# First scores on other banks, fewer stack transfers, two sets of q and k parts, first row sums on PE, calls reordered

## The chip, the cores and the metric

The kernel runs on one core of one Trainium2 chip. The metric is the device time of one execution in microseconds; lower is better. Engines are called PE (TensorE), ACT (ScalarE), DVE (VectorE), POOL (GpSimd) and SP (SyncE, which here only issues DMAs). All engines run side by side and wait for each other on semaphores.

## The reference, cut to what matters

A transformer block with modulated norms, in float32, for x of 8 batches x 512 rows x 256 columns: windowed causal attention with 16 heads of 16 (a row sees itself and the 128 rows before it), a GELU block of width 1024, and a mixing block.

```python
mod = (silu(c) @ wmod).reshape(B, 6, 1, -1)          # sa, ca, ga, sb, cb, gb
h = layernorm(x) * (1 + ca) + sa
# attention block on h
a = layer_norm(h, ln1_w, ln1_b)
q, k, v = (a @ W + b).reshape(B, L, 16, 16)
scores = einsum("blhd,bmhd->bhlm", q, k) / 4 + band   # -inf outside 0 <= i - j <= 128
ctx = einsum("bhlm,bmhd->blhd", softmax(scores), v)
h = h + ctx @ Wo + bo
h = h + gelu(layer_norm(h, ln2_w, ln2_b) @ W1 + b1) @ W2 + b2
x = x + ga * h                                        # |ga| is held at 0.25 or more
# mixing block
h = layernorm(x) * (1 + cb) + sb
prev = h shifted by one row
r = sigmoid((mu_r * h + (1 - mu_r) * prev) @ W_r.T)
k = square(relu((mu_k * h + (1 - mu_k) * prev) @ W_k.T))
out = x + gb * (r * (k @ W_v.T))
```

## The kernel before

There are 8 batches (`n` or `b`) and 16 half batches. In the attention part a half batch `u` is half of the heads (8 of 16, all 512 rows); in the later parts a half batch `i` is half of the rows (256). Each engine has its own block of code with functions such as `scores(gp, first, last_)`, and then a long list of calls: the order of work on each engine is written out by hand, call by call, with a loop over batches 3 to 6 (DVE and POOL have their own bounds) in the middle. Engines only meet on semaphores. A call of a half batch that doesn't exist does nothing.

The attention of a half batch goes like this. `norm_a` (ACT) and `transposes_a` (PE) bring the normed rows into `at_hi` and `at_lo`, two float16 parts of one float32 value. `project(u)` (PE) makes q and k. `high_qk(u)` (ACT) and `low_qk(u)` (DVE) split them into `qt_hi`, `qt_lo`, `kt_hi`, `kt_lo`; k has a pair of columns for each row, one for the even and one for the odd head, so that a pair of heads shares 32 partitions. `maxima(u, 0..3)` takes all four banks of `quad`: PE multiplies the high parts alone, DVE reduces them to a bound of the row's maximum (`nmax`). `max_rows`, `max_copy`, `low_m` and `max_send` (PE, ACT, DVE, ACT's DMA) bring that into four rows of the stack `q_st`. `stacks(u, first, last_)` are DMAs from SBUF to SBUF: for each of four pairs `j` they put the parts of q and of k on top of each other, so that one product over 96 + 4 rows gives high x high + low x high + high x low less the maximum. Before, each pair takes six DMAs (three of q, three of k), and ACT issues the pairs 2 and 3 of the first two half batches, SP all others. The stacks have two buffers (`half`), the parts have one.

`scores(gp, first, last_)` (PE), with gp = 4u + j, writes four pieces, each to a bank of the ring `ring_s`, which are the four banks of `quad`; `exps` (ACT) takes the exponential of two of them at a time into one of eight `p32`; `select(gp)` (POOL) sets what lies outside the band to zero; `sums(gp)` (POOL) adds the overlapping parts of a row into `ps` (two additions). `context(u)` (PE) multiplies by the values (`v_blk`) into bank 4 and then sums the rows with `sel` into the bank `den`. `copy_den` (ACT), `fold_den`, `save_den`, `spread_den` (SP's DMAs) and `divide`, `scale_c` (DVE) apply 1/sum. Two half batches of `scale_c` complete a batch of `ct`; then `out_project`, `residual_a`, `stats_b`, `rstd_b`, `norm_b`, `transposes_b`, `up`, `gelu`, `high_f`, `low_f`, `down` and the mixing block (`transposes_d`, `receptance`, `keys`, `values_b` on PE) follow, on the rings `ring_b` (banks 6 and 7) and `ring_f` (bank 5).

A ring hands out its banks in turn, and a new user waits for the semaphore of the bank's last user. `load_v(n, half)` fills half of `v_blk` with four DMAs. `warm(n, times)` are products of the identity with itself into bank 5, whose results nobody reads. The weights are prepared at the start by the functions `setup_...`. `hold` is a wait that is left out where an earlier wait of that engine covers it.

## Time and profile before

| | us |
|---|---|
| median of 3 runs (643.40 to 646.79) | 643.89 |
| the profiled execution | 644.62 |
| its span, first to last instruction | 642.9 |
| PE busy | 579.4 (90%), 6494 products |
| DVE busy | 418.7 (65%) |
| ACT busy | 449.8 (70%) |
| POOL busy | 384.1 (60%) |
| mean granted clock of PE | 0.975 of 2.4 GHz |

How to read it: products on PE overlap, so PE busy is not PE at its peak. The filler products of `warm` count as busy (L229, 322 products, 49.7 us, two for each `times`). The share of busy time is an average over a start in which the weights are prepared and the first batches come in, a repeating middle and an end. DMAs are not in the busy times; a "q" behind an engine's name (SPq, ACTq) is its issuing side.

### The profile page before, as it was taken

Reading aid. Unit: us, or ns where it says so; the run is one execution under the profiler, and the core shown is the slowest. Engines: PE = TensorE matmul, PEld = TensorE weight load, DVE = VectorE, ACT = ScalarE, POOL = GpSimd, SP = SyncE. Lnnn points to the kernel's source line nnn. Section 1 sums busy time; section 2 is a strip of 40 time slices with the busy share of each in tenths; the row PEclk is TensorE's granted clock in tenths of the full one; section 3 lists DMA queues with packets and bytes.
Section 4 is the critical chain, followed back from the end, with each engine's and each line's share of the span. In section 5 each row is a group of like instructions: output and inputs, shape, how many; then the busy total and the mean of one; then the engine's idle time right before and its main releaser. Section 6 shows DMA issues by size and latency. Waiting matters only on the chain.

```text
span 642.9 us, 16628 instructions
## 1 busy us (share of the span) xinstructions
PE 579.4 (90%) x6494; PEld 454.9 (71%) x6494; DVE 418.7 (65%) x847; ACT 449.8 (70%) x758; POOL 384.1 (60%) x610
## 2 busy tenths in 40 slices
PE   5888888799889999989998999999899989999986
...
GB/s 239 194 92 128 84 58 52 86 68 102 112 115 53 79 57 69 124 91 104 57 136 83 112 44 112 108 114 47 94 97 95 51 97 44 93 36 34 34 42 33
DMA packets 63516, 55.74 MB, mean 87 GB/s; under 512 B 14459, under 2 KB 52669, under 8 KB 63438
## 3 DMA queue, kind: packets, MB, share of 16 engines
...
q14 instruction: 27, 0.22, 0.1%
...
## 4 chain that ended last, share of the span: by engine, by line
PE 52%; DVE 16%; ACT 14%; SPq 5%; POOL 5%; issue 4%; DMA 3%; ACTq 0%; DVEq 0%; POOLq 0%
PE bank L351 4%; DVE nmax L1519 4%; PE bank L468 4%; PE quad L330 3%; PE bank L456 3%; PE bank L480 3%; PE bank L429 3%; PE bank L430 3%; PE bank L431 3%; PE quad L380 3%; PE bank L229 3%; ACT bank L1021 3%; SPq L2536 2%; SPq L2538 2%; PE quad L257 2%
## 5 line engine op out<-in xcount | busy, mean ns | idle before, releaser
L970 ACT ACTIVATE p<-quad,scale_s 128x768 f32<-128x768 f32 (+1 forms) x90 | 73.3, 825 | 17.4 <-PE quad L330 16.0
L2151 POOL TENSOR_SCALAR_AFFINE_SELECT p<-p 128x448 f32<-128x448 f32 x64 | 40.3, 630 | 73.9 <-ACT p L975 45.6
L1519 DVE TENSOR_REDUCE nmax<-quad 128x8 f32<-128x1032 f32 x64 | 78.9, 1233 | 2.2
L1021 ACT ACTIVATE bank<-bank,bias,scale_g 128x256 f32<-128x256 f32 x128 | 63.1, 532 | 17.3 <-PE bank L414 17.1
L412 PE MATMUL bank<-bt_hi,w_hi 128*128 128x256 f16 x256 | 70.3, 275 | 4.1 <-DVE hid_lo L1579 4.0
L429 PE MATMUL bank<-w_hi,hid_hi 128*128 128x256 f16 x256 | 69.9, 273 | 1.4 <-DVE hid_lo L1579 0.9
L413 PE MATMUL bank<-bt_lo,w_hi 128*128 128x256 f16 x256 | 69.9, 273 | 0.0
L414 PE MATMUL bank<-bt_hi,w_lo 128*128 128x256 f16 x256 | 69.8, 273 | 0.0
L431 PE MATMUL bank<-w_hi,hid_lo 128*128 128x256 f16 x256 | 69.8, 273 | 0.0
L430 PE MATMUL bank<-w_lo,hid_hi 128*128 128x256 f16 x256 | 69.8, 273 | 0.0
L2166 POOL TENSOR_TENSOR ps<-p 128x384 f32<-128x384 f32 x64 | 65.2, 1019 | 3.1 <-PE quad L363 1.3
L330 PE MATMUL quad<-q_st,k_st 100*128 100x192 f16 (+3 forms) x576 | 57.7, 231 | 9.9 <-ACT p L970 4.4
L1579 DVE SCALAR_TENSOR_TENSOR hid_lo<-bank,inv_f,hid_hi 128x512 f16<-128x512 f32 x64 | 47.2, 745 | 21.8 <-ACT hid_hi L1031 21.4
L2168 POOL TENSOR_TENSOR ps<-ps,p 128x320 f32<-128x320 f32 x64 | 56.9, 889 | 5.0
L330 PEld LDWEIGHTS quad<-q_st,k_st 100*128 100x128 f16 x576 | 41.2, 98 | 23.3 <-issue 5.1
L975 ACT ACTIVATE p<-quad,scale_s 128x288 f32<-128x288 f32 (+1 forms) x76 | 36.8, 541 | 19.8 <-PE quad L330 19.7
L1516 DVE COPY_PREDICATED quad<-later,quad 128x248 f32<-128x248 int16 x64 | 26.7, 416 | 36.7 <-PE quad L296 36.6
L229 PE MATMUL bank<-ident 128*128 128x128 f32 x322 | 49.7, 309 | 0.3 <-DVE peak L1732 0.3
L229 PEld LDWEIGHTS bank<-ident 128*128 128x128 f32 x322 | 44.2, 216 | 3.1 <-issue 1.1
L1031 ACT ACTIVATE hid_hi<-bank,inv_f 128x512 f16<-128x512 f32 x64 | 43.4, 688 | 3.8 <-PE bank L431 1.6
L1506 DVE SCALAR_TENSOR_TENSOR kt_lo<-kc,pick,kt_hi 128x512 f16<-128x512 f32 x32 | 26.9, 894 | 25.5 <-ACT kc L936 25.5
L351 PE MATMUL bank<-p,v_blk 128*32 128x192 f32 (+2 forms) x1024 | 41.5, 316 | 0.6 <-POOL p L2156 0.3
...
## 6 DMA issues: line engine op xcount, KB each, us to landing
v_blk<-vn SPq DMA_DIRECT2D x64, 128.0 KB, 2.6
k_st<-kt_hi SPq DMA_DIRECT2D x120, 64.0 KB, 2.0
...
q_st<-qt_hi SPq DMA_DIRECT2D x120, 32.0 KB, 1.9
...
```

What stands on the lines that cost most here:

```text
L229: e.matmul(psum[5][:, 0:P], ident[:, :], ident[:, :], start=True, stop=True)
L330: last = e.matmul(bank[:, c0:c0 + w], k_st[0:MR, half, j, s * P:(s + 1) * P], q_st[0:MR, half, j, s * KW + q0:s * KW + q0 + w], start=True ...
L351: e.matmul(bank[32 * j:32 * j + 32, s * KW:s * KW + w], v_blk[:, half, s, 2 * j * HD:2 * (j + 1) * HD], p32[(4 * u + j) % SLOTS][:, c:c + ...
L412: e.matmul(dst, w1_hi[:, k, ms], bt_hi[:, k, :], start=(k == 0), stop=False)
L413: e.matmul(dst, w1_hi[:, k, ms], bt_lo[:, k, :], start=False, stop=False)
L414: last = e.matmul(dst, w1_lo[:, k, ms], bt_hi[:, k, :], start=False, stop=(k == KC - 1))
L429: e.matmul(dst, hid_hi[:, m, ts], w2_hi[:, m, :], start=(m == 0), stop=False)
L430: e.matmul(dst, hid_hi[:, m, ts], w2_lo[:, m, :], start=False, stop=False)
L431: last = e.matmul(dst, hid_lo[:, m, ts], w2_hi[:, m, :], start=False, stop=(m == MF - 1))
L970: e.activation(p32[gp % SLOTS][:, c0:c0 + 2 * w].rearrange("p (n c) -> p n c", n=2), quad[:, b0:b0 + 2, 0:w], ACT.Exp, scale=scale_s[:, 1: ...
L1021: e.activation(dst, dst, ACT.Gelu_apprx_tanh, bias=bias_1[:, m:m + 1], scale=scale_g[:, 0:1]).then_inc(s_gl, 1)
L1519: e.tensor_reduce(nmax[:, :, :, qt].rearrange("p a j -> p j a"), quad[:, :, 2 * QB - 2:2 * WIN].rearrange("p j (c a) -> p j a c", a=2), AX ...
```

## The change

Five things change, and the order of calls on all engines with them.

1. Two sets of parts: `q_two[i]` and `k_two[i]` (i = u % 2) hold high and low side by side. `high_qk(u)` waits for `maxima` and stacks of u - 2 in place of u - 1.
2. `stacks` has four DMAs a pair, 16 a half batch, in place of six and 24: the rows of high and low q come from one DMA, the doubled k from one with a broadcast source. All are issued by SP; the function goes from ACT. Each buffer of stacks has its own semaphores.
3. The scores of gp < 12 (`APART`, u = 0 to 2) go to the ring `ring_e`, banks 5 and 6, in place of the four banks of `quad`. The fillers up to number 19 go to bank 4, from number 20 on to bank 5 and they wait for the last exponential of u = 2. `transposes_b(0)`, the first user of `ring_b`, waits for it too.
4. For u < 2 (`DIRECT`) `context` sums the rows by 32 products of `sel` with `p32`; `sums` of these eight groups goes from POOL.
5. `v_blk` and `vn` have another layout, `load_v(n)` fills all of `v_blk` with two DMAs and waits for `context(2n - 1)`.

In the setup the fixed banks of some small products change, `setup_modt` and `setup_mod_cols` are parted from `setup_gates` and `setup_mod_rest`, and some waits are put elsewhere. `warm` is called for 131 products of the identity in place of 161: 89 before `context(0)` in both, 42 in place of 72 after it.

```diff
-        qt_hi, qt_lo = sb("qt_hi", [P, L], F16), sb("qt_lo", [P, L], F16)
-        kt_hi, kt_lo = sb("kt_hi", [P, 2 * L], F16), sb("kt_lo", [P, 2 * L], F16)
+        q_two, k_two = [sb(f"q_two_{i}", [P, 2, L], F16) for i in range(2)], [sb(f"k_two_{i}", [P, 2, 2 * L], F16) for i in range(2)]
...
+        ring_e = Banks(psum[5:7])
+        ring_q = [ring_e] * APART + [ring_s] * (NG - APART)
...
 def warm(n, times):
                 if n == 0:
                     e.wait_ge(s_pool, POOL_IDENT)
-                    e.wait_ge(s_peak, 3)
+                if n == WARM:
+                    e.wait_ge(s_ex, 2 * APART)
...
 def scores(gp, first, last_):
-                    bank, free = ring_s.take(("st", gp, i), s_ex, 2 * gp + i // 2 + 1)
+                    bank, free = ring_q[gp].take(("st", gp, i), s_ex, 2 * gp + i // 2 + 1)
...
-                        e.wait_ge(s_stk[j], 6 * DMA * (u + 1))
+                        e.wait_ge(s_stk[half][j], 4 * DMA * (u // 2 + 1))
...
 def context(u):
-                e.wait_ge(s_sm, 4 * (u + 1))
                 hold(e, *free)
+                if u < DIRECT:
+                    for s in (0, 3, 6, 1, 2, 4, 5, 7):
+                        c, w = {6: (6 * QW, 2 * KW), 7: (6 * QW + 2 * KW, KW)}.get(s, (s * QW, QW))
+                        for j in range(HQ):
+                            last = e.matmul(den[32 * j:32 * j + 32, s * KW:s * KW + w], sel[:, :], p32[(4 * u + j) % SLOTS][:, c:c + w],
+                                            start=(s == 0), stop=(s == 7))
+                    last.then_inc(s_av, 1)
+                    return
+                e.wait_ge(s_sm, 4 * (u + 1 - DIRECT))
...
 def high_qk(u):
-                hold(e, s_mxm, 4 * u)
+                hold(e, s_mxm, 4 * (u - 1))
                 for j in range(HQ):
-                    hold(e, s_stk[j], 6 * DMA * u)
+                    hold(e, s_stk[m][j], 4 * DMA * (u // 2))
...
 def stacks(u, first, last_):
-                    for r, part in enumerate((qt_hi, qt_lo, qt_hi)):
-                        e.dma_start(q_st[2 * HD * r:2 * HD * (r + 1), half, j, :], part[src, :]).then_inc(s_stk[j], DMA)
-                    for r, part in enumerate((kt_hi, kt_hi, kt_lo)):
-                        e.dma_start(k_st[2 * HD * r:2 * HD * (r + 1), half, j, :], part[src, :]).then_inc(s_stk[j], DMA)
+                    e.dma_start(q_st[0:4 * HD, half, j, :], q_two[half][src, :, :]).then_inc(s_stk[half][j], DMA)
+                    e.dma_start(k_st[0:4 * HD, half, j, :], k_two[half][src, 0:1, :].broadcast_to([2 * HD, 2, 2 * L])).then_inc(s_stk[half][j], DMA)
+                    e.dma_start(q_st[4 * HD:SR, half, j, :], q_two[half][src, 0, :]).then_inc(s_stk[half][j], DMA)
+                    e.dma_start(k_st[4 * HD:SR, half, j, :], k_two[half][src, 1, :]).then_inc(s_stk[half][j], DMA)
...
 def sums(gp):
-                if not 0 <= gp < NG:
+                if not 4 * DIRECT <= gp < NG:
...
-            def load_v(n, half):
+            def load_v(n):
                 e.wait_ge(s_v3, 4 * (n + 1))
-                hold(e, s_av, 2 * n - 1 + half if n else 0)
-                for a in range(2):
-                    for i in range(2):
-                        e.dma_start(v_blk[a:P:2, half, i:8:2, :], vn[KW * i:KW * (i + 1), :, a, half, :]).then_inc(s_vin[half], DMA)
+                hold(e, s_av, 2 * n)
+                for i in range(2):
+                    e.dma_start(v_blk[:, i, :, :, :], vn[KW * i:KW * (i + 1), :, :, :, :]).then_inc(s_vin, DMA)
```

The new order of calls, where it matters most. PE:

```
maxima(1, 0)  warm  maxima(1, 1)  scores(0, 2, 4)  warm  scores(1, 0, 2)  warm
maxima(1, 2)  setup_mod_cols  maxima(1, 3)  scores(1, 2, 4)  scores(2, 0, 2)
transposes_a(1)  max_rows(1)  scores(2, 2, 4)  scores(3, 0, 2)  project(2)
values(1, 0)  scores(3, 2, 4)  warm  scores(4, 0, 2)  maxima(2, 0)  setup_f1
scores(4, 2, 4)  warm  scores(5, 0, 2)  maxima(2, 1)  context(0)
```

ACT at the start: `norm_a(0)`, `setup_wqk`, `high_a(0)`, `setup_wv`, `high_qk(0)`, `load_ones`, `setup_sq1`, `max_copy(0)`; before, `load_ones` stood behind `norm_a(0)`. SP: `load_w2` and `load_rest` (w_mod, w1 and the mixing weights) stand behind `load_x(1)` and `load_mod_a(1)`, where they stood before them; then

```
stacks(0, 0, 2)  rows_bias  load_mod_a(2)  load_v(0)  stacks(0, 2, 4)
stacks(1, 0, 2)  rows_gates  load_x(2)  stacks(1, 2, 4)  stacks(2, 0, 2)
stacks(2, 2, 4)  fold_den(0)  save_den(0)  spread_den(0)  fold_den(1)
save_den(1)  spread_den(1)  load_v(1)  load_x(3)  stacks(3, 0, 2)  fold_den(2)
load_residual(0)  load_mod_g(0)  stacks(3, 2, 4)  save_den(2)  spread_den(2)
load_mod_a(3)  stacks(4, 0, 2)  fold_den(3)  stacks(4, 2, 4)  save_den(3)
```

## Rows read from the trace of the kernel before

**Rows 1.** Windows: busy us (instructions) of each engine, clock, DMA share, GB/s.
```profile
83.90:110.70 26.80, 22.82 (x280) 17.31 (x273) 17.58 (x40) 9.90 (x16) 18.76 (x27) 0.81 0.21 55
110.70:136.90 26.20, 21.61 (x261) 16.95 (x254) 13.48 (x26) 16.47 (x28) 15.46 (x25) 0.87 0.32 88
136.90:167.70 30.80, 29.32 (x389) 24.06 (x384) 18.35 (x35) 25.73 (x41) 19.24 (x30) 1.00 0.34 91
167.70:199.50 31.80, 28.41 (x364) 22.19 (x361) 25.37 (x47) 24.24 (x42) 22.89 (x36) 0.95 0.40 109
...
388.70:455.50 66.80, 62.63 (x754) 48.59 (x754) 48.96 (x99) 54.87 (x94) 44.92 (x72) 1.00 0.34 94
```

**Rows 2.** The same windows for L229, the fillers, alone: PE, PEld, clock, DMA.
```profile
83.90:110.70 26.80, 4.13 (x20) 3.23 (x20) 0.81 0.21 55
110.70:136.90 26.20, 7.30 (x40) 6.34 (x40) 0.87 0.32 88
136.90:167.70 30.80, 9.26 (x70) 8.28 (x70) 1.00 0.34 91
167.70:199.50 31.80, 1.81 (x14) 1.64 (x14) 0.95 0.40 109
```

**Rows 3.** The chain that ended last, 113 to 168 us, shares by line.
```profile
by line: SPq L2536 28.6%; SPq L2538 26.0%; DMA rc<-dn 10.3%; DMA k_st<-kt_lo 7.5%; issue 6.6%; ACT kt_hi L934 6.2%; SPq L2547 4.6%; DMA den_rows<-rc 4.5%; SPq L2567 2.3%; ACT kc L936 1.9%; DVE kt_lo L1506 1.4%; DVE rc L1532 1.3%; ACT dn L95
```

**Rows 4.** Timeline of SP's issues: start us, us, what; first and last of two groups.
```profile
116.94 0.61 SPq L2536 DMA_DIRECT2D q_st<-qt_hi  x1
...
132.49 0.62 SPq L2538 DMA_DIRECT2D k_st<-kt_lo  x1
...
146.18 0.57 SPq L2536 DMA_DIRECT2D q_st<-qt_hi  x1
...
162.66 0.59 SPq L2538 DMA_DIRECT2D k_st<-kt_lo  x1
```

**Rows 5.** SP's issues of k, whole span: ns min/median/max, first and last start.
```profile
L2538 SPq DMA_DIRECT2D k_st<-kt_hi x120: 516/591/1859, 35.7 to 537.5; - x120
```

**Rows 6.** Timeline of ACT at 165 us; in brackets idle before and releaser.
```profile
164.83 0.69 ACT L931 ACTIVATE qt_hi<-quad,bias_q 128x512 f16<-128x512 f32 x1 [2.49 <-DMA k_st<-kt_lo]
```

**Rows 7.** Timeline of ACT, 20 to 64 us.
```profile
20.20 3.23 ACTq L1145 DMA_DIRECT2D k_st<-k_st  x4
...
63.87 0.89 ACT L975 ACTIVATE p<-quad,scale_s 128x288 f32<-128x288 f32 x2 [10.13 <-PE quad L330]
```

**Rows 8.** Timeline of PE, 26 to 84 us.
```profile
26.85 0.38 PE L257 MATMUL quad<-at_hi,wa_hi 128*128 128x512 f16 x1 [1.51 <-DVE wa_lo L1760]
...
49.73 0.49 PE L330 MATMUL quad<-q_st,k_st 100*128 100x192 f16 x4
...
63.53 0.43 PE L330 MATMUL quad<-q_st,k_st 100*128 100x192 f16 x5 [0.73 <-DVE nmax L1519]
...
77.09 2.94 PE L229 MATMUL bank<-ident 128*128 128x128 f32 x24
...
80.40 2.49 PE L351 MATMUL bank<-p,v_blk 128*32 128x192 f32 x64
82.67 0.86 PE L356 MATMUL quad<-ps,sel 128*32 128x384 f32 x8
```

**Rows 9.** The page: one group (count, busy us, mean ns, idle) and one DMA line.
```profile
L970 ACT ACTIVATE p<-quad,scale_s 128x768 f32<-128x768 f32 (+1 forms) x90 | 73.3, 825 | 17.4 <-PE quad L330 16.0
...
v_blk<-vn SPq DMA_DIRECT2D x64, 128.0 KB, 2.6
```

**Rows 10.** A window of the weights' loads: length, clock, DMA share, GB/s.
```profile
16.00:20.00 4.00, 1.00 1.04 416
```

**Rows 11.** Timeline of POOL: first selection, the sums behind it, the second selection.
```profile
64.83 0.61 POOL L2151 TENSOR_SCALAR_AFFINE_SELECT p<-p 128x448 f32<-128x448 f32 x1 [15.94 <-ACT p L975]
...
66.21 0.99 POOL L2166 TENSOR_TENSOR ps<-p 128x384 f32<-128x384 f32 x1
...
68.10 0.60 POOL L2151 TENSOR_SCALAR_AFFINE_SELECT p<-p 128x448 f32<-128x448 f32 x1
```

968 lines of the change are left out of this document (457 added, 511 removed).

## The prediction

> **What bounds the kernel now.** Put windows over the work first. In the repeating middle the granted clock of TensorE (PE) stays at its upper level, 2.4 GHz; before about 200 us it falls several times to 1.2 GHz, so that windows there show 0.81 or 0.87 [rows 1]. In that middle a batch takes 66.8 us and PE is busy for 62.6 of them (two more such windows, before and after the one shown, give 62.6 as well; it is the last line of [rows 1]): nothing is left there but some 4 us of small gaps, so the middle is bound by PE. The start is not. I cut it where the attention product of a half batch ends on PE (I call these marks C0 to C4: 83.9, 110.7, 136.9, 167.7 and 199.5 us). Between C0 and C4 lie 115.6 us with PE busy for 102.2 [rows 1], but 22.5 of these are filler products with the identity, `warm`, whose results nobody reads [rows 2]. So PE does 79.7 us of work in 115.6. A half batch needs 33.4 us in the middle, and four of them take 115.6 us here although PE has about 36 us to spare: something else sets the pace.
>
> The chain of waits for 113 to 168 us says what [rows 3]: 54.6% of it is the SP queue issuing stack transfers (L2536, L2538), 7.5% the landing of the last of them. The queue itself shows it: 24 issues from 116.94 to 133.1 us, then 24 more from 146.18 to 163.25 [rows 4], about 0.63 us apart. ScalarE (ACT) waits for exactly these before it may overwrite the single set of q and k parts: its `high_qk(5)` starts at 164.83 on the landing of the last `k_st` transfer, after 2.49 us of idling [rows 6], and `high_qk(4)` at 134.65 did the same. Behind `high_qk` stands `copy_den` on ACT, behind that `fold_den` on SP, and behind that the next 24 issues. That is a loop of SP and ACT, 28 to 30 us a turn.
>
> At the very start two things stand out. ACT issues four transfers of ones (3.23 us) between `norm_a(0)` and `high_a(0)` [rows 7], and the first projection starts at 26.85 [rows 8]. Then the first two pieces of scores run at 49.73, but the next two only at 63.53 [rows 8]: they share the four banks of `quad` with `maxima(1, ...)`, and ACT idles 10.13 us for them [rows 7].
>
> **Stack transfers, two sets of parts.** Per half batch 24 issues become 16. At 0.63 us that is 10.1 us in place of 15.1, and in the new order `fold_den(2)` and `fold_den(3)` stand between the first and the second eight, so a fold waits behind 8 issues, 5 us, not behind 24. No row has an issue with a broadcast source of this form. Its price lies between 0.59 us, the median of the k issues, and 1.86, the longest of them [rows 5]; I take 0.63, as bytes and rows per partition stay the same. With the broadcast four at the upper end a half batch costs 4.9 us more on SP, 15.0, as much as before. With two sets, `high_qk(u)` waits for the stacks of u - 2. This wait goes, in [rows 6] and in its like. What is late next is PE itself or POOL: `context(2)` needs `select(8)` to `select(11)` and their sums, which my walk below puts at 119 us, the last thing that it waits for.
>
> The whole of `v_blk` is loaded at once, two issues of 512 KB for 8 of 128 KB [rows 9]. The wait is stronger: `load_v(n)` waits for `context(2n-1)`, where half 0 could start a context earlier. Queued behind it on SP are the next stacks. A context is 26 to 33 us from the next, the transfer lands in under 5 us by the rate of [rows 10] and 2.6 us for the old piece, so it is covered; if the cover went, `context(2n)` on PE would wait and 3 to 5 us a batch would be lost.
>
> For u = 0 and 1 ACT no longer issues half the stacks: SP has all 16. The first eight need 5 us from about 31 us on and are wanted at 46; the other eight wait behind `load_v(0)` until about 53 and are wanted at 57. I cost this at nothing. The weights w2, w_mod 1 and 2, w1 and the mixing weights (about 3.8 MB) now queue behind `load_x(1)`, which waits for the first transposes at 21.6. At 416 GB/s [rows 10] that is 9 us, so w1 lands near 36 and everything near 38; `setup_sq1` on ACT is then 2 us late with 2 us to spare. At half that rate the first stacks land near 46 and 1 to 4 us of the start are lost.
> The Trainium skill, page DMA: Bandwidth & Descriptors, section Issuing engines are not separate DMA queues, says that issuing from several engines saves only the sequencer's issue time, since all transfers share the same engines. That speaks against taking the stacks off ACT: here it is the issue time that stands in the chain [rows 3], so by the rule dropping ACT as issuer gives some back, at most 8 issues or 5 us for each of u = 0 and 1 if nothing covered them, and the result would be about 640.
>
> **Scores on two other banks** (u = 0 to 2). `scores(0, 2, 4)` no longer waits for `maxima(1, 3)`. The walk through the first 75 us, each step with its old duration: ones out of ACT's way, project(0) starts 2.0 us earlier (24.8, where the split of the weights is next); `setup_exp`, `scale_x(1)` and `shift_x(1)` leave DVE's path between the four maxima, so that the first scores come at 46.0, 3.7 us earlier; `scores(0, 2, 4)` then follow `maxima(1, 1)` at about 51, 12 us earlier; POOL starts selecting at 54, not at 64.83 [rows 11]. `context(0)` starts at 73.6 where it started at 80.40 [rows 8].
>
> **Row sums on PE alone** (u = 0 and 1). Removed: 8 pairs of POOL additions, 8 x 1.89 = 15.1 us (66.21 to 68.10 [rows 11]), which lay ahead of the selections. Added: the denominators take 32 products like those of the value part, 2.3 us by the row of L351 (80.40 to 82.67), in place of 1.2 (82.67 to 83.9) [rows 8]; +1.1 us on PE twice. So C0 comes at 78.4, 5.5 us earlier.
>
> **C0 to C4.** Two accounts. PE's: fillers after `context(0)` fall from 72 to 42; 30 x 0.24 us (12 of them took 2.94 at 2.4 GHz [rows 8]) = 7.2 us. If PE's gaps of 13.4 us [rows 1] and the cost of half clock stay as they were, C4 comes 5.5 + 7.2 - 1.1 = 11.6 us earlier (of the two 1.1 one is in the 5.5). The walk's, with every wait followed: C1 at 97 (ahead of it are exps in a row, setup_bias and project(3)), C2 at 120.5 (POOL's sums), C3 at 149.5, C4 at 180 or 181; 19 us earlier. The walk gives every hand-over its best case. I take 14, nearer to PE's account, since it is closed at both ends by rows.
>
> **After C4** the order changes only in neighbours (scores and transposes_a swapped, a step up or down). SP and the DMA engines, busy to 0.34 [rows 1], bind nothing there, so I take zero, within 1.5 us either way, and the shift of 14 is carried to the end. Sum: span 642.9 - 14 = 628.9; the profiled execution had 644.62 with 1.7 us around its span, and the median of the runs is 643.89; from that, 629.9, say 630.
>
> **Rivals.**
> A, the walk is right: 19 us, 625. For it: the loop of [rows 3] is wholly gone. Against: five hand-overs in a row at their best.
> B, only the front gains: C0's 5.5 us and little more, 637. POOL's sums of u = 2 stand in a block ahead of `context(2)`, 1.38 for a selection and 1.89 for the sums [rows 11] of each of four groups, and could take the place of the SP queue.
> C, the clock: with 30 fillers fewer PE idles more and falls to 1.2 GHz for longer. The stage from 83.9 to 110.7 had a granted clock of 0.81, the mean of the four stages is 0.91 [rows 1]. If all four had 0.81, 0.10 x 115.6 = 11.6 us would be lost of the 14: 641. Against: the fillers go where real work now comes. The Trainium skill, page TensorE: Matmul & The Clock Gate, section HAM oscillation, how this bites in real kernels, has it that waits for data put the array back to its low clock again and again; [rows 1] agree for the start, and by the rule 641 would be the time.
> D, slower. Two banks tie PE to ACT: each of the 24 half groups of u = 0 to 2 needs both banks, so it may not start before the exponentials of the one before are done, 0.83 us [rows 9] and two hand-overs, 1.2 us, while PE stands in order. With four banks PE was one half group ahead. Nine pairs stand next to each other in the new order and are in my walk; if the other 15 stall too, that is 18 us, and 630 + 18 = 648. It decides from 12 of these 15 on (14 us). Against: most have a projection, maxima or fillers between.
> E, no effect: the gain is swallowed by gaps before C4, 644.
>
> **Chances.** Forecast (11 to 17 us) 0.39, A 0.22, B 0.19, C 0.06, E 0.04, D 0.10. Half a per cent, 3.2 us, is about what can be told from no change. Faster by more: forecast, A, B and a part of C, 0.82; within: 0.08; slower: 0.10. The range leaves out D, E, C: 621 (A with the middle's 1.5 and some more) to 640 (B with weights late).
>
> **What would show it.** C0 at 78, C1 at 97 to 101, C4 near 185; 66.8 us a batch after it. SP: 16 issues in about 10 us and no wait of ACT's L931 for `k_st`. POOL's first selection at 54. Wrong: L931 of ACT still waiting for a transfer (the second set of parts buys nothing); C1 early but C4 not (B, look for POOL ahead of L356); granted clock under 0.9 from C0 to C4 (C); PE idle ahead of L330 after ACT, over 1 us more than twelve times (D); issues of `k_st` at 1.9 us (SP as slow as before).

## The result and the profile after

The changed kernel takes 640.15 us in the median of 20 executions (635.95 to 643.54), the kernel before, run beside it, 644.57 (640.43 to 647.0). The ratio is 0.9933, 95% interval 0.991 to 0.9956: 0.7% or 4.3 us faster, where 14 us (630, range 621 to 640) were forecast. The profiled execution took 638.1 us, 2 us less than the median, with a span of 635.0 us (642.9 before) and a mean granted clock of 0.973 (0.975). So the leads in the table are about 2 us larger than the medians show. One execution further down (of e1_mid, 1141.8 us) was a disturbed one and enters no figure.

The table gives the ends of the context products on PE in the two profiled executions, and the prediction's two numbers.

| end of context | C0 | C1 | C2 | C3 | C4 | C6 | C12 | C15 |
|---|---|---|---|---|---|---|---|---|
| before | 84.0 | 110.8 | 137.0 | 167.7 | 199.6 | 274.9 | 475.3 | 565.7 |
| after | 82.6 | 105.6 | 128.5 | 157.2 | 189.4 | 266.1 | 468.1 | 558.9 |
| lead | 1.4 | 5.2 | 8.5 | 10.5 | 10.2 | 8.8 | 7.2 | 6.7 |
| predicted by the walk | 78.4 | 97 | 120.5 | 149.5 | 180 to 181 | | | |
| taken for the sum | 78.4 | | | | 185.5 | lead kept | lead kept | lead kept |

Against the walk the time went in three places: 4.2 us before C0, 4.4 more between C0 and C1, and 3.5 after C4, where I had expected nothing. Between C1 and C4 the walk was right to 1 us. In the middle a batch takes 67.4 us (C6 to C12, three batches, 202.1 us) where it took 66.8.

The stages of after, cut at its own marks C0 to C4, and one stretch of 66.8 us of its middle answer to [rows 1]; the columns are busy us (instructions) of PE, its weight loads, DVE, ACT, POOL, then clock, DMA share, GB/s.

```profile
82.60:105.60 23.00, 21.29 (x242) 16.27 (x243) 8.58 (x15) 12.18 (x19) 6.22 (x16) 0.70 0.15 39
105.60:128.50 22.90, 17.24 (x254) 12.13 (x254) 15.28 (x35) 12.77 (x19) 15.57 (x26) 0.85 0.41 110
128.50:157.20 28.70, 27.83 (x369) 22.43 (x369) 20.89 (x42) 24.97 (x39) 16.83 (x28) 1.00 0.28 77
157.20:189.40 32.20, 28.37 (x379) 23.51 (x376) 18.63 (x28) 23.31 (x40) 21.46 (x31) 0.95 0.45 117
383.00:449.80 66.80, 61.83 (x753) 48.45 (x753) 47.29 (x96) 54.49 (x92) 46.67 (x74) 1.00 0.35 91
```

The first line is the one to stop at. Between C0 and C1 PE is busy for 21.29 of 23.0 us, and DVE, ACT and POOL for less than 13 each. PE alone sets the pace, at a granted clock of 0.70 of 2.4 GHz: 13.8 of these 23 us are at 1.2 GHz. What that costs is seen in the 32 products of `setup_bias` (L561), which take 6.99 us here and 3.73 at 2.4 GHz in e3_fill, a kernel described below (L565 there):

```profile
86.51 6.99 PE L561 MATMUL rest<-col,stage 128*128 128x1 f32 x32
```
```profile
90.15 3.73 PE L565 MATMUL rest<-col,stage 128*128 128x1 f32 x32
```

No filler runs between C0 and C1; the fillers (L235 now) in the same stages, as [rows 2]:

```profile
82.60:105.60 23.00, 0.00 (x0) 0.00 (x0) 0.70 0.15 39
105.60:128.50 22.90, 0.71 (x4) 0.52 (x4) 0.85 0.41 110
128.50:157.20 28.70, 9.01 (x66) 7.91 (x66) 1.00 0.28 77
157.20:189.40 32.20, 1.81 (x14) 1.64 (x14) 0.95 0.45 117
```

The loop of SP and ACT is gone, as the prediction had it. In the page's chain of the whole span SP has 1%; what has come up is POOL:

```profile
PE 45%; POOL 17%; DVE 13%; issue 10%; ACT 10%; DMA 4%; SPq 1%; ACTq 0%; POOLq 0%; DVEq 0%
```

SP issues the third x only at 64.42 us, in the middle of an unbroken row of stack transfers (the columns are start us, us, what):

```profile
61.98 0.60 SPq L2487 DMA_DIRECT2D k_st<-k_two  x1
...
63.26 0.60 SPq L2489 DMA_DIRECT2D k_st<-k_two  x1
63.90 0.48 SPq L2570 DMA_DIRECT2D mod_rows<-x  x1
64.42 0.40 SPq L2466 DMA_DIRECT2D xa<-x  x1
64.93 0.59 SPq L2486 DMA_DIRECT2D q_st<-q_two  x1
```

And DVE waits for it, with `low_qk(2)` (L1492, L1496) and the first maxima of u = 2 (L1506, L1509) standing behind it (timeline of DVE; in brackets the idle time ahead and what ended it):

```profile
69.15 1.41 DVE L1437 BATCH_NORM_STATS2 st_x<-xa 128x6 f32<-128x256 f32 x4 [4.18 <-DMA xa<-x]
70.47 0.36 DVE L1440 BATCH_NORM_AGGREGATE mv_x<-st_x 128x2 f32<-128x6 f32 x4
70.87 1.67 DVE L1459 SCALAR_TENSOR_TENSOR h<-xa,mv_x,mod_a 128x256 f32<-128x256 f32 x4
72.46 0.74 DVE L1492 SCALAR_TENSOR_TENSOR q_two<-quad,bias_q,q_two 128x512 f16<-128x512 f32 x1
73.12 1.46 DVE L1496 SCALAR_TENSOR_TENSOR k_two<-kc,pick,k_two 128x512 f16<-128x512 f32 x2
74.48 0.41 DVE L1506 COPY_PREDICATED quad<-later,quad 128x248 f32<-128x248 int16 x1
```

On PE the front's marks, against [rows 8]: the first scores at 47.76, the next two pieces at 52.73 (63.53 before), 26 fillers, then `context(0)` at 77.81 with its row sums (L364) at 80.11:

```profile
47.76 0.50 PE L338 MATMUL rest<-q_st,k_st 100*128 100x192 f16 x4
...
52.73 0.43 PE L338 MATMUL rest<-q_st,k_st 100*128 100x192 f16 x5
...
74.12 3.15 PE L235 MATMUL rest<-ident 128*128 128x128 f32 x26
...
77.81 2.49 PE L357 MATMUL rest<-p,v_blk 128*32 128x192 f32 x64
80.11 2.46 PE L364 MATMUL quad<-p,sel 128*32 128x192 f32 x64
```

### The profile page after: what moved, and what is told of

It reads as the page before. It is cut to its first block, busy times and chain, and to the rows that moved or that the text cites. A ratio compares the mean times of both kernels' runs of the same rounds, so it can differ in the third digit from the quotient of the medians.

```text
span 635.0 us, 16439 instructions
## 1 busy us (share of the span) xinstructions
PE 571.3 (90%) x6498; PEld 447.6 (70%) x6498; DVE 413.1 (65%) x847; ACT 448.2 (71%) x750; POOL 364.2 (57%) x594
## 4 chain that ended last, share of the span: by engine, by line
PE 45%; POOL 17%; DVE 13%; issue 10%; ACT 10%; DMA 4%; SPq 1%; ACTq 0%; POOLq 0%; DVEq 0%
PE rest L357 4%; POOL ps L2159 3%; PE rest L482 3%; PE rest L494 3%; PE rest L470 2%; PE quad L338 2%; ACT p L976 2%; PE rest L443 2%; PE rest L235 2%; PE rest L444 2%; PE rest L445 2%; POOL p L2144 2%; DVE hid_lo L1569 2%; PE rest L426 2%; POOL ps L2161 2%
## 5 line engine op out<-in xcount | busy, mean ns | idle before, releaser
L1509 DVE TENSOR_REDUCE nmax<-quad 128x8 f32<-128x1032 f32 x64 | 78.9, 1234 | 2.2
L426 PE MATMUL rest<-bt_hi,w_hi 128*128 128x256 f16 x256 | 70.4, 275 | 6.0 <-DVE hid_lo L1569 5.9
L1027 ACT ACTIVATE rest<-rest,bias,scale_g 128x256 f32<-128x256 f32 x128 | 63.4, 533 | 16.2 <-PE rest L428 16.0
L443 PE MATMUL rest<-w_hi,hid_hi 128*128 128x256 f16 x256 | 69.9, 273 | 0.9 <-DVE hid_lo L1569 0.9
L428 PE MATMUL rest<-bt_hi,w_lo 128*128 128x256 f16 x256 | 70.1, 274 | 0.0
L427 PE MATMUL rest<-bt_lo,w_hi 128*128 128x256 f16 x256 | 70.1, 274 | 0.0
L445 PE MATMUL rest<-w_hi,hid_lo 128*128 128x256 f16 x256 | 69.8, 273 | 0.0
L444 PE MATMUL rest<-w_lo,hid_hi 128*128 128x256 f16 x256 | 69.8, 272 | 0.0
L1569 DVE SCALAR_TENSOR_TENSOR hid_lo<-rest,inv_f,hid_hi 128x512 f16<-128x512 f32 x64 | 46.8, 743 | 18.9 <-ACT hid_hi L1037 18.7
L1506 DVE COPY_PREDICATED quad<-later,quad 128x248 f32<-128x248 int16 x64 | 26.7, 417 | 32.6 <-PE quad L303 32.5
L1037 ACT ACTIVATE hid_hi<-rest,inv_f 128x512 f16<-128x512 f32 x64 | 43.8, 687 | 3.9 <-PE rest L445 1.6
L357 PE MATMUL rest<-p,v_blk 128*32 128x192 f32 (+2 forms) x1024 | 39.8, 307 | 1.1 <-POOL p L2149 1.1
L357 PEld LDWEIGHTS rest<-p,v_blk 128*32 128x32 f32 x1024 | 32.0, 110 | 11.6 <-issue 6.1
L1496 DVE SCALAR_TENSOR_TENSOR k_two<-kc,pick,k_two 128x512 f16<-128x512 f32 x32 | 25.5, 850 | 17.2 <-ACT kc L943 17.2
```

The lines of the kernel that those rows point to most:

```text
L357: e.matmul(bank[32 * j:32 * j + 32, s * KW:s * KW + w], v_blk[:, s % 2, s // 2, half, 2 * j * HD:2 * (j + 1) * HD], p32[(4 * u + j) % SLOT ...
L426: e.matmul(dst, w1_hi[:, k, ms], bt_hi[:, k, :], start=(k == 0), stop=False)
L427: e.matmul(dst, w1_hi[:, k, ms], bt_lo[:, k, :], start=False, stop=False)
L428: last = e.matmul(dst, w1_lo[:, k, ms], bt_hi[:, k, :], start=False, stop=(k == KC - 1))
L443: e.matmul(dst, hid_hi[:, m, ts], w2_hi[:, m, :], start=(m == 0), stop=False)
L444: e.matmul(dst, hid_hi[:, m, ts], w2_lo[:, m, :], start=False, stop=False)
```

## How the experiments are compared

Each ratio is to the kernel before, measured beside it on the same chip. Inside the traces I count from the start of `project(1)`, which varies by itself: kernels with the same first 20 us have it between 40.05 and 43.86. A good part of the reason is visible: in some executions the clock is at 1.2 GHz for a part or all of 16 to 22 us, in others not, though PE is busy for 6.00 of the 6.00 us from 10 to 16 in all of them. Window 16 to 22 us of e6_dve, then of e8_front, which have the same work there (here and below: length, PE busy us and instructions, clock, DMA share, GB/s):

```profile
16.00:22.00 6.00, 4.40 (x28) 1.00 0.02 3
```
```profile
16.00:22.00 6.00, 6.00 (x13) 0.50 0.02 3
```

The second execution was slower a little earlier too: its four products of 128x512 at 10.40 us take 2.60 us, those of e6_dve at 10.02 take 1.88. With 1.00 there, `project(0)` starts at 24.2 to 24.7 in the changed kernels and at 26.8 to 27.0 with the start of before; with the lower clock at 26.4 to 27.6 and at 28.0. The 2.0 us that I gave to the ones leaving ACT's path are real, but an execution's own clock moves as much. One profile is therefore good to 2 or 3 us (C0 of e15_apart8 comes 3.0 later than that of after, although its edit lies behind C0), and a ratio to 0.3%. The profiled executions of e8_front and e9_direct0 took 2 us more than the medians of their kernels and that of after 2 us less; this is why the last columns and the ratio need not agree.

| end of context, us after project(1) starts | C0 | C1 | C2 | C3 | C4 | C6 | C12 | C15 | ratio (95%) |
|---|---|---|---|---|---|---|---|---|---|
| before | 39.6 | 66.4 | 92.6 | 123.4 | 155.2 | 230.5 | 430.9 | 521.3 | 1 |
| after | 40.7 | 63.7 | 86.6 | 115.4 | 147.6 | 224.2 | 426.3 | 517.1 | 0.9933 (0.991 to 0.9956) |
| e4_both | 41.2 | 68.1 | 94.3 | 124.2 | 153.8 | 229.2 | 429.5 | 520.2 | 0.9953 (0.9926 to 0.9981) |
| e13_two | 41.1 | 68.0 | 92.6 | 122.5 | 153.8 | 229.1 | 429.3 | 520.1 | 0.9987 (0.9962 to 1.0012) |
| e14_16 | 39.7 | 65.3 | 90.3 | 120.2 | 149.8 | 225.1 | 425.4 | 515.8 | 0.9968 (0.9944 to 0.9992) |
| e17_nowarm | 41.2 | 71.1 | 98.5 | 128.4 | 158.0 | 233.4 | 433.7 | 523.7 | 1.0027 (1.0003 to 1.0051) |
| e18_nowarm0 | 41.2 | 71.2 | 98.6 | 128.5 | 158.1 | 238.8 | 439.3 | 529.6 | 1.0091 (1.006 to 1.0122) |
| e15_apart8 | 43.7 | 65.2 | 95.0 | 123.9 | 156.4 | 234.0 | 436.0 | 526.8 | 1.0067 (1.0037 to 1.0097) |
| e9_direct0 | 39.9 | 60.3 | 89.1 | 117.8 | 149.0 | 227.0 | 430.5 | 521.2 | 0.9913 (0.9885 to 0.994) |
| e7_weights | 41.5 | 61.4 | 87.0 | 115.7 | 145.9 | 223.9 | 425.9 | 516.6 | 1.0005 (0.9982 to 1.0028) |
| e5_mid2 | 40.6 | 63.6 | 86.6 | 115.3 | 147.5 | 224.3 | 424.6 | 516.7 | 0.9892 (0.9859 to 0.9926) |
| e3_fill | 44.5 | 63.0 | 88.2 | 116.9 | 149.5 | 226.1 | 428.8 | 519.6 | 0.9932 (0.9907 to 0.9956) |
| e6_dve | 40.1 | 61.6 | 87.6 | 116.4 | 146.9 | 224.8 | 426.9 | 517.7 | 0.9888 (0.9858 to 0.9918) |
| e8_front | 41.5 | 61.6 | 84.3 | 113.1 | 145.5 | 223.5 | 427.0 | 517.8 | 0.9863 (0.9844 to 0.9882) |
| e10_den | 35.5 | 57.6 | 80.2 | 109.0 | 141.2 | 219.1 | 422.4 | 513.2 | 0.9842 (0.9819 to 0.9865) |
| e11_best | 35.6 | 59.3 | 81.9 | 110.7 | 142.6 | 219.3 | 419.6 | 511.7 | 0.9816 (0.9791 to 0.9842) |
| e12_nofill | 36.6 | 61.6 | 84.5 | 115.5 | 148.6 | 225.3 | 425.5 | 517.5 | 0.9889 (0.986 to 0.9917) |
| e16_best2 | 35.6 | 59.0 | 81.6 | 110.4 | 142.6 | 219.3 | 419.5 | 511.5 | 0.9832 (0.9793 to 0.9872) |

## What the stack edits give: e4_both, e13_two, e14_16

In the kernel before, its order kept, either the second set of parts, or 16 transfers, or both (e13_two has the first two lines of the diff, e14_16 the others with one set; k likewise).

```diff
-        qt_hi, qt_lo = sb("qt_hi", [P, L], F16), sb("qt_lo", [P, L], F16)
+        q_two = [sb(f"q_two_{i}", [P, 2, L], F16) for i in range(2)]
...
-                    for r, part in enumerate((qt_hi, qt_lo, qt_hi)):
-                        e.dma_start(q_st[2 * HD * r:2 * HD * (r + 1), half, j, :], part[src, :])
+                    e.dma_start(q_st[0:4 * HD, half, j, :], q_two[u % 2][src, :, :])
+                    e.dma_start(q_st[4 * HD:SR, half, j, :], q_two[u % 2][src, 0, :])
```

> The kernel before, in its own order, with only the two sets of q and k parts and 4 DMAs a pair (16 a half batch) in place of 6; ACT still issues half of them for u = 0 and 1; scores, row sums, v_blk and fillers as before. Theory 'stack loop': the loop of SP and ACT that the chain of waits showed from 113 to 168 us set the pace, so that taking it away gives 4 to 8 us by context 4 (ends at 192 to 196 in place of 199.6), total 636 to 640 (0.988 to 0.994). Rival 'order': with before's order and its fillers PE, POOL and DVE are nearly as late as SP; expected within 1.5 us of before, 643 to 644.5 (0.998 to 1.0).

> The kernel before with the second set of q and k parts alone; still 24 transfers a half batch. e4_both (two sets and 16 transfers) had context 3 0.8 us and context 4 3.1 us ahead of the kernel before, and held 3.1 us to the end (ratio 0.9953). Theory 'the set': ACT's wait for the last k_st goes, so this kernel has the same 3 us (0.994 to 0.996). Rival 'the issues': SP still needs 15 us for 24 issues and sets the pace; within 1 us of before (0.999 to 1.001).

> The kernel before with 4 DMAs a pair (16 a half batch, two of them with both parts in one) and one set of parts. Theory 'the issues': a turn of the loop of SP and ACT is 5 us shorter, which is more than PE can use; 2 to 3 us faster (0.995 to 0.997). Rival 'the set': high_qk still waits for the last transfer; within 1 us of before (0.999 to 1.001).

Both together give 3.0 us (0.9953, with an interval that allows 1.2 to 4.8). By their times neither single edit differs clearly from both (0.9987 and 0.9968, the intervals overlap), and the second set alone isn't told from no change either (0.9962 to 1.0012), so how the 3 us are shared stays open; in the traces either one alone brings at least as much by C4 as both. That fits a loop of two links of which either may be shortened: with one set and 16 transfers, as with two sets and 24, `high_qk` no longer waits for a transfer. In the kernel before it did so only twice between 28 and 205 us, for 3.1 us in all. The chain of e4_both from 113 to 168 us, against [rows 3], shows what was next in line:

```profile
by line: PE bank L228 23.4%; PE quad L330 11.5%; PE bank L351 8.8%; PE quad L380 6.5%; DVE nmax L1523 4.5%; PE bank L412 3.5%; DMA rc<-dn 3.4%; PE quad L296 3.3%; PE bank L413 3.2%; PE bank L414 3.2%; PE quad L257 3.1%; PE quad L258 3.1%; P
```

SP's 54.6% are gone, and the first item is L228, the fillers. The loop had been taken for the pace; PE with its fillers was 3 us behind it.

## What fillers are worth: e17_nowarm, e18_nowarm0

The 30 double fillers (two products each) between contexts 0 and 2 (numbers 20 to 32) removed, from e4_both and from the kernel before.

```diff
             scores(6, 0, 2)
-            warm(20, 2)
             scores(6, 2, 4)
-            warm(21, 2)
             scores(7, 0, 2)
...
-            warm(30, 7)
-            warm(31, 1)
```

> e4_both (the kernel before with two sets and 16 transfers) without the fillers numbered 20 to 32, 30 double products between contexts 0 and 2. With SP's loop gone, a quarter of the chain from 113 to 168 us is fillers (L228). Theory 'fillers on the path' (PE's account in the prediction, 7.2 us for 30): contexts 2 to 4 end 4 to 7 us earlier than in e4_both, ratio 0.985 to 0.990. Rival 'clock': without them PE idles and stays at 1.2 GHz for longer, which takes it back; within 1.5 us of e4_both, ratio 0.993 to 0.998, or slower.

> The kernel before without the same 30 double fillers, nothing else. Theory 'SP paces' (rows of the chain): the fillers stand in PE's slack there and nothing is gained, within 1 us of before (0.999 to 1.001), or 1 to 4 us lost by the clock (1.002 to 1.006). Rival 'PE paces': fillers delay PE already in the kernel before; 3 to 7 us faster (0.989 to 0.995).

Both are slower without them: by 0.74% against e4_both (1.0027 to 0.9953) and by 0.91%, 5.9 us, against before. The window 84 to 137 us of before, then of e18_nowarm0:

```profile
84.00:137.00 53.00, 44.43 (x528) 0.84 0.27 71
```
```profile
84.00:137.00 53.00, 36.75 (x417) 0.73 0.22 60
```

7.7 us of busy PE went and the clock fell from 0.84 to 0.73, 5.8 us of full speed in 53. A double filler here doesn't cost 0.24 us, it earns some: in e17_nowarm the loss against e4_both is 4.2 us at C2 and still 4.2 at C4, 0.14 for each. This is rival C's mechanism. The Trainium skill, page TensorE: Matmul & The Clock Gate, section HAM oscillation, has waits put the array back to its low clock, and both lines agree. The 5.9 us of e18_nowarm0 are not the clock's alone. It is 6.0 us behind the kernel before at C2, 2.9 at C4 and 8.3 at C6. Up to C4 it is equal to e17_nowarm (158.1, 158.0), then that is 5.4 us ahead: with 24 stack transfers a half batch SP issues the next x only at 200.86 us, DVE waits 5.31 us for it with `low_m` behind, and PE 2.38 us for the maxima that follow; e17_nowarm, with 16, has none of these waits. This bears out the stack edits, and it is the same fault, a load behind a row of stack transfers, as at the front of the changed kernel.

## The two banks: e15_apart8

```diff
-    APART = 12
+    APART = 8
```

> The changed kernel with the scores of u = 2 (groups 8 to 11) on the four banks of quad again, in the new order; only those of u = 0 and 1 on the two other banks. Theory 'two banks bind PE': after context 1 two banks make PE idle 0.5, 0.5, 0.9 and 0.8 us ahead of scores for ACT's exponentials; with four banks context 2 ends 1 to 2.5 us earlier (84 to 85.6 after the start of project(1), 86.6 in the changed kernel) and the end 1 to 2 us, 0.990 to 0.992. Rival 'shared with maxima': the groups then wait for DVE's maxima of u = 3 on the same banks, as before the change; context 2 ends 0 to 3 us later, 0.993 to 0.997.

Rival D is refuted with its sign: with u = 2 back on the four shared banks, context 2 ends 8.4 us later (6.9 of them lie between C1 and C2, where the edit acts) and the whole is 1.3% slower than the changed kernel, slower than the one before. In the changed kernel itself PE waits for ACT ahead of scores on the two banks 7 times, 4.8 us in all and never over 1.0, where D wanted more than twelve waits of over 1 us. In e15_apart8 PE waits ahead of scores for DVE's maxima instead (timeline of PE):

```profile
109.48 0.66 PE L338 MATMUL quad<-q_st,k_st 100*128 100x192 f16 x5 [1.99 <-DVE nmax L1509]
...
117.29 1.30 PE L338 MATMUL quad<-q_st,k_st 100*128 100x192 f16 x9 [1.85 <-DVE nmax L1509]
...
127.58 0.43 PE L338 MATMUL quad<-q_st,k_st 100*128 100x192 f16 x5 [1.85 <-DVE nmax L1509]
```

The separate banks carry the new order. That the same holds for u = 0 and 1 wasn't tried: as I read the waits, in this order those groups can't go back to the shared banks without PE and DVE waiting for each other for good.

## The row sums: e9_direct0

```diff
-    DIRECT = 2
+    DIRECT = 0
...
             select(0)
+            sums(0)
```
(and so for groups 1 to 7)

> The changed kernel with the row sums of u = 0 and 1 on POOL again (two additions a group right behind its selection, 8 x 1.9 us) and 16 products of ps for each context on PE as in later ones. Theory 'not needed': in the changed kernel POOL idles 9.8 and 9.0 us ahead of select(7) and select(8), so its sums fit in there, and each of the first two context products is 1.1 us shorter; contexts 1 to 4 end within 1 us of the changed kernel's, total 639.5 to 641 (0.993). Rival, as the prediction had it: the sums stand ahead of selections that context 0 waits for, context 0 ends 3 to 5 us later and the end 2 to 4 us, 642 to 644 (0.996 to 0.999).

0.9913 against 0.9933: the edit gives nothing that can be told. Contexts 0 and 1 even come earlier with POOL's sums, since PE has 16 products where it had 32; after C1 that kernel falls back (89.1 at C2). I had priced the removed additions at 15.1 us "ahead of the selections"; with the scores early, POOL idles in between anyway.

## Weights behind load_x(1): e7_weights

```diff
-            load_x(1)
-            load_mod_a(1)
             load_w2()
             load_rest()
+            load_x(1)
+            load_mod_a(1)
```

> The changed kernel, but SP issues w2, the rest of w_mod, w1 and the mixing weights ahead of load_x(1), not behind it. In the changed kernel setup_mod_rest waits 1.86 us on PE until 35.11 and setup_sq1 8.85 us on ACT until 38.60 for them. Theory 'weights late': these waits go, scores(0, 0, 2) come 1 to 2 us earlier than 47.76, and the end 0.5 to 2 us earlier, 638 to 639.5 (0.990 to 0.993). Rival: they were covered (as the prediction put it), and x of batch 1 comes later instead; 640 to 641 (0.993 to 0.995).

The opposite: 0.7% slower than the changed kernel. With the weights ahead, the second x comes late, and `low_qk(0)` stands behind it on DVE (timelines of DVE, then PE, in e7_weights):

```profile
33.08 1.41 DVE L1437 BATCH_NORM_STATS2 st_x<-xa 128x6 f32<-128x256 f32 x4 [5.31 <-DMA xa<-x]
```
```profile
35.51 0.29 PE L299 MATMUL quad<-k_two,q_two 32*32 32x256 f16 x16 [3.93 <-DVE q_two L1492]
```

So the weights' new place isn't "covered at nothing": it protects the order of DVE, for 4 to 5 us (1.0005 against 0.9933).

## The order of the middle: e1_mid, e2_midpool, e5_mid2

The order of calls of before on all engines, or on POOL alone, from group 24 to the end of batch 7's values. On POOL for one batch:

```diff
 select(28)
-rstd_c(3)
-first_column(3)
+bias_h(7)
+sums(28)
 select(29)
-sums(28)
 scale_o(2)
+sums(29)
 select(30)
-sums(29)
```

> The changed kernel, with the order of calls of the kernel before on all five engines from about 225 us (the scores of group 24) to the end of batch 7's values (about 505 us); start and end as changed. In the traces the lead over the kernel before falls from 8.8 us at the end of context 5 to 7.0 at the end of context 13. Theory 'order': the new order of the middle costs this; expected 1.8 us faster than the changed kernel, about 638.3 (ratio to before 0.990). Rival 'start': a deficit carried over from the start, or transfers (512 KB of v_blk at once, broadcast sources), costs it, whatever the order; expected 640.1 (0.993).

> The kernel of e1_mid once more: its time was the changed kernel's within the interval (ratio 0.9947 against 0.9933), where theory 'order' wanted 0.990, but its profiled execution was a disturbed one (1139 us), so the stages weren't to be seen. Theory 'order': the lead at the ends of contexts 5 and 13 is the same, 8.8 us and 8.8, where the changed kernel has 8.8 and 7.0, and context products wait 0 for POOL's selection in the middle (0.4 us each time after). Rival 'start': 8.8 and 7.0 as in the changed kernel.

> As e1_mid, but only POOL has the order of before in the middle; the other four engines keep the new one. Theory 'POOL': the context products wait for POOL (1.1 us in the middle after, 0 before), so POOL's order alone gives e1_mid's result, 638.3. Rival: the small changes on PE, ACT and DVE (keys and scores waiting 2.3 and 2.5 us on DVE after, 1.0 and 1.5 before) do it, and POOL's order alone gives 640 or more, up to 642 as the orders no longer fit each other.

The two measurements of the same kernel give 0.9947 (0.992 to 0.9975) and 0.9892; the first has no usable trace. By the times no gain is shown: they lie on both sides of 0.9933. The traces show one for the stretch itself: with before's order the lead over before is 9.2 us at C6 and 9.3 at C12, with the new one 8.8 and 7.2. It isn't one execution's chance: from C6 to C12 the four traces with before's middle (e5_mid2, e11_best, e12_nofill, e16_best2) take 200.2 to 200.3 us, as before (200.4), the eight with the new one 202.0 to 203.5. In the new order context products wait for POOL's selections and `keys` for DVE (groups of PE from 300 to 475 us, after; the last column is idle before and its cause):

```profile
L357 PE MATMUL rest<-p,v_blk 128*32 128x192 f32 (+2 forms) x320 | 12.4, 307 | 0.7 <-POOL p L2149 0.7
...
L482 PE MATMUL rest<-mixed,wb 128*128 128x256 f32 x40 | 9.9, 391 | 1.7 <-DVE mixed L1602 1.7
```

In e5_mid2 the first of them has no idle time:

```profile
L357 PE MATMUL rest<-p,v_blk 128*32 128x192 f32 (+2 forms) x320 | 12.4, 307 | 0.0
```

So the order costs 2 us by C12. At the seam behind C12 e5_mid2 loses 1.5 of them again, and at C15 it leads the changed kernel by 0.8. The 1.4 us that go between C4 and C5 lie ahead of the part that was exchanged. There the changed kernel has a wait that the kernel before hasn't: `transposes_b(2)` on PE waits for `norm_b(2)` of ACT, which the new order puts behind `exps(20, ...)`; before, it stood ahead of `copy_den(4)` and was done in time (PE of after, ACT of after, ACT of before):

```profile
199.13 0.66 PE L407 MATMUL rest<-ident,nrm_b 128*128 128x128 f32 x4 [1.87 <-ACT nrm_b L1007]
```
```profile
198.00 1.08 ACT L1007 ACTIVATE nrm_b<-x,nb_b,rs_b 128x256 f32<-128x256 f32 x2
```
```profile
197.34 1.09 ACT L1001 ACTIVATE nrm_b<-x,nb_b,rs_b 128x256 f32<-128x256 f32 x2 [0.47 <-POOL nb_b L2131]
```

POOL has what `norm_b(2)` needs at 193.3 us, so it is the order of ACT that makes it late. Putting it back wasn't tried. e2_midpool is 1.0105: POOL's old order among the others' new ones costs 11 us, so a POOL order is only good or bad with the orders around it.

## Clock and order at the front: e3_fill, e6_dve, e8_front, e10_den, e12_nofill

e3_fill has 41 more double fillers in PE's gaps (14 and 27 by its list of calls; the expectations below say 43), in bank 4 and in an unused part of bank 7:

```diff
+            warm(13, 6)
             maxima(1, 1)
...
+            warm_7(8)
             maxima(3, 2)
```

> The changed kernel with 43 more filler products of the identity put where PE idled in its trace before, at 51, 59, 63, 83 to 86, 106 to 111, 113 and 119 us (and setup_f2 on PE a few calls later). Theory 'clock': three stretches at half clock (58.1 to 68.3, 85.4 to 99.0, 109.3 to 116.1 us, 30.6 us together) hit dense work and cost up to 15 us of full speed work; with the gaps filled at least the second is gone: context 1 ends 4 to 6 us earlier (100 to 102 in place of 105.6), and the total is 634 to 637 (ratio 0.984 to 0.988). Rival 'hand-overs': PE waits for DVE and ACT there, and the clock only decides how fast it reaches the next wait; expected 639.5 to 641 (0.993). Fillers that come too long: up to 642.

The clock did what it should (0.89 in place of 0.78 from 60 to 125 us, the first line is after, the second e3_fill), and the time didn't change:

```profile
60.00:125.00 65.00, 56.17 (x685) 0.78 0.35 90
```
```profile
60.00:125.00 65.00, 55.98 (x729) 0.89 0.35 90
```

`project(2)` was done at 65.89 and not at 69.23, and then DVE idled 6.13 us for x. From C0 to C1 it needed 18.5 us at a clock of 0.91, the walk's 18.6, but C0 came 3.8 us later, with fillers at half clock ahead of it, and C1 only 0.7 earlier (from `project(1)`). So the clock was one half; e6_dve takes the other:

```diff
 low_m(1)
+low_qk(2)
+maxima(2, 0)
 stats_x(2)
 scale_x(2)
-low_qk(2)
-maxima(2, 0)
```
(on POOL, select(3) ahead of rstd_x(2))

> The changed kernel with three calls moved: on DVE low_qk(2) and maxima(2, 0) stand ahead of stats_x(2), as before the change, and on POOL select(3) ahead of rstd_x(2). In the changed kernel DVE idles 4.18 us for the third x, which SP issues only at 64.42 us, behind 16 stack transfers, and low_qk(2) stands behind that. Theory 'x transfer': low_qk(2) comes 2 us earlier (70 to 72.5), context 0 ends 1 to 2 us earlier (81), and the total is 638.5 to 639.5 (0.991); no more, since fillers and half clock stand ahead of it too. Rival 'clock': project(2) at half clock (64.7 to 69.2) and the fillers (74.1 to 77.3) set context 0 by themselves; no change, 82.6 and 640 (0.993).

0.9888 (0.9858 to 0.9918), not clear of the changed kernel's 0.9933 (0.991 to 0.9956), and C0 only 0.6 us earlier from `project(1)`: PE now waits inside `context(0)`, for the bank of the row sums, 1.60 us. e8_front has both edits and 3 double fillers ahead of `context(0)` where there were 12 (nine fewer, 2.2 us at 0.24 each, in all kernels that follow):

> The fillers of e3_fill and the reordering of e6_dve together, and 3 in place of 12 double fillers ahead of context(0). In e3_fill project(2) was done 3.3 us earlier (65.9 in place of 69.2), and then DVE idled 6.13 us for x. Theory 'both': each alone only uncovers the other; together context 0 ends at 77 to 79 (the 78.4 of the prediction), context 1 at 96 to 99, and the total is 634 to 636 (0.984 to 0.987). Rival 'later': the lead is lost again before context 2 (POOL's sums, the transfers of the denominators), so that context 2 ends at 127 to 129 as in the changed kernel and the total is 639 to 640 (0.992).

0.9863 (0.9844 to 0.9882), clear of the changed kernel, the ratio of the first theory but not its C0 and C1: C1, C2 and C4 are 2 us earlier than in the changed kernel, C0 isn't. The same wait has grown (timelines of PE, then DVE, in e8_front):

```profile
80.81 3.81 PE L368 MATMUL quad<-p,sel 128*32 128x192 f32 x64 [3.50 <-DVE nmax L1858]
```
```profile
75.70 1.67 DVE L1808 SCALAR_TENSOR_TENSOR h<-xa,mv_x,mod_a 128x256 f32<-128x256 f32 x4
77.49 1.67 DVE L1817 SCALAR_TENSOR_TENSOR h<-h,rs_x,mod_a 128x256 f32<-128x256 f32 x4
79.08 0.41 DVE L1855 COPY_PREDICATED quad<-later,quad 128x248 f32<-128x248 int16 x1
79.52 1.23 DVE L1858 TENSOR_REDUCE nmax<-quad 128x8 f32<-128x1032 f32 x1
```

The bank is freed by `maxima(2, 1)`, which stands behind two operations on the third x that nobody needs yet. e10_den puts it ahead:

```diff
+maxima(2, 1)
 scale_x(2)
 shift_x(2)
-maxima(2, 1)
```

> e8_front with one more call moved: on DVE maxima(2, 1) ahead of scale_x(2) and shift_x(2). In e8_front the second half of context 0, the row sums on PE, waited 3.50 us for the bank that DVE's maxima(2, 1) frees, at 80.75, behind scale_x and shift_x. Theory 'den bank': counted from the start of project(1), context 0 ends 3 to 3.5 us earlier than in e8_front (38 us in place of 41.5) and context 1 by 2 to 3 (59); the end at best 1 to 2 us earlier, ratio 0.982 to 0.985. Rival: context 2 stays where it is (84.3 us after project(1)), since the transfers of the denominators and POOL's selections and sums come in between; ratio 0.986 as e8_front.

By the traces the first theory holds, and was too modest: C0 comes 6.0 us earlier than in e8_front (3.5 are the wait), C1 4.0 and C2 still 4.1. The ratio, 0.9842, is clear of the changed kernel's but not of e8_front's. From the changed kernel's start of `project(1)` (41.88) its C0 would be at 77.4, C1 at 99.5, C2 at 122.1, C4 at 183.1: the walk had 78.4, 97, 120.5, 180 to 181. The nine double fillers fewer are a part of that, for the changed order, which the walk followed, has them. From C0 to C1 it needs 22.0 us, at a clock of 0.85: PE now waits 2.08 us there for `setup_f1` of DVE, so with C0 early the clock is only a part of what the walk had too short.

e11_best adds the order of the middle, e12_nofill is the same without the 41 fillers, and e16_best2 also has `setup_f1()` on DVE ahead of `scale_x(2)`.

> e10_den's start and e1_mid's middle (before's order of calls from batch 3 to 7). In e5_mid2 the middle kept its lead of 9.2 us from context 6 to 12, where the changed kernel loses 1.6 of its 8.8; in e8_front the lead fell from 11.0 at context 4 to 5.1 at context 13, so there is more to keep. Theory 'order of the middle': ratio 0.979 to 0.983 (630 to 633 us). Rival: the loss stands between contexts 4 and 5 (2.7 us in e8_front), ahead of the part that is exchanged; 0.984 to 0.987.

> e11_best without the 43 added filler products (setup_f2 back at its place), the reordering of DVE and POOL and of the middle as there. Theory 'clock': the fillers keep 2.4 GHz through project(2), transposes_a(2), out_project(0) and project(4), 2 to 4 us by context 3; this one is 2 to 4 us slower than e11_best. Rival: what the clock gives back is waited away; within 1 us of e11_best.

> e11_best with one more call moved: on DVE setup_f1 ahead of scale_x(2). In e11_best the fillers behind context 0 waited 2.08 us for it (until 80.22), and the clock fell behind that. Theory: context 1 ends 2 to 4 us earlier (56 to 57 after the start of project(1), 59.3 in e11_best), the clock stays at 2.4 GHz through setup_bias, and the end is 1 to 2 us earlier, ratio 0.978 to 0.981. Rival: DVE's work is only exchanged and nothing gained, 0.9816 as e11_best.

e11_best is the fastest kernel of this study, 631.74 us, 0.9816: 1.8% faster than before and 1.2% faster than the changed one. Its gain over e10_den isn't shown by the times (0.9842, the intervals overlap), only by the stretch from C6 to C12. Without the fillers 0.7%, 4.7 us, are lost (0.9889): in the right order they pay, where in e3_fill they didn't. From 60 to 125 us, e11_best and then e12_nofill:

```profile
60.00:125.00 65.00, 59.72 (x829) 0.92 0.35 91
```
```profile
60.00:125.00 65.00, 54.05 (x703) 0.82 0.35 91
```

e16_best2 gave nothing further (0.9832, the intervals overlap; C1 0.3 us earlier), as its rival had it.

## Why the prediction was wrong, point by point

**The start, 5.5 us predicted, 1.4 measured.** The gain that there is lies ahead of `project(1)` (44.38 before, 41.88 after; e4_both, e13_two and e14_16, with the start of before, have 42.58 to 43.60); from there to C0 the changed kernel needs 40.7 us and the kernel before 39.6. The first scores came at 47.76 (46.0 predicted), the next at 52.73 (51), POOL's first selection at 55.90 (54): all 2 us late, and part of that is `setup_mod_rest` waiting 1.86 us on PE for w_mod. The step that failed is `context(0)` at 73.6; it started at 77.81. The walk moved `setup_exp`, `scale_x(1)` and `shift_x(1)` out of DVE's path, but didn't see that the same new order puts `stats_x(2)` and `scale_x(2)` ahead of `low_qk(2)`, behind a transfer. And "SP has all 16 ... I cost this at nothing" left `load_x(2)` out, which is queued behind them: x may be loaded from 62.5 us on, when `transposes_a(1)` ends, and is issued at 64.42, 1.9 us late. The Trainium skill's rule that I set against it (page DMA: Bandwidth & Descriptors, section Issuing engines are not separate DMA queues: another issuer saves only issue time) named just this price, and I looked for it at the stacks, not at the load behind them.

**C0 to C4, 8.5 us by the sum (14 less 5.5), 8.8 measured.** The total is right by accident. Of the walk's 13 to 14 us for this stretch 4.4 were lost between C0 and C1, a stage with PE busy for 21.29 of 23.0 us at 0.70; `setup_bias` alone has 3.3 of them by the clock (6.99 for 3.73 us). PE's account had the term 30 x 0.24 = 7.2 us for fillers left out. Its sign is wrong, as far as it was tried in before's order: when they go, 0.7%, 4.8 us, are lost with the stack edits in place (e17_nowarm), and 5.9 without, a part of which is the late x. "If PE's gaps and the cost of half clock stay as they were" was the condition, and it doesn't hold, for the fillers are what keeps the clock. Rival C had the mechanism and 641 us; it got 0.06 because "the fillers go where real work now comes", while the clock fell in the changed kernel at 85 us, behind context 0 and three gaps of only 0.36, 0.36 and 0.99 us. That its 641 is so near is luck, though: over the four stages the granted clock is 0.89, just under its sign of 0.9, where C had 0.81. The full speed lost to it is about 12 us in 106.8, against 10 in 115.6 before, so 2 us more and not 11.6.

**Stack transfers and two sets.** The loop was real and is gone, 16 issues of 0.60 us, broadcast source (L2487) included, the lower end of my range; but it was worth 3 us, not the pace of four contexts: PE with its fillers stood right behind it. `v_blk` in one piece lands in 6.0 us in the median, over the 5 that I had, and was covered all the same: no context product waits for it.

**Scores on two other banks.** Right, and the edit on which the new order rests (6.9 us between C1 and C2 in e15_apart8, 1.3% in all). Rival D failed.

**Row sums on PE.** +1.1 us on PE twice as predicted (2.46 us for L364, where 2.3 were worked out); the 15.1 us taken from POOL bought nothing (e9_direct0).

**The middle, zero predicted, 3.5 us lost from C4 to C15.** "The order changes only in neighbours" was read off PE's list. POOL's and ACT's lists changed too, and with PE busy for 62 of 67 us a context that waits 0.4 us for a selection shows. Of the 3.5 us, 1.4 went by C5, where `norm_b(2)` came late on ACT; before's order of the middle keeps the next 2 up to C12, and 0.8 of them at C15 (e5_mid2).

**The method.** Taking 14 between two accounts looked careful, but both had the same two holes. The walk was good where it was checked engine by engine; e10_den, with nine double fillers fewer, reaches it within 1 us at C0 and 3 at C4. What the walk lacked is the transfer in front of DVE, the bank in the middle of context 0, and a clock.
